# Selective-scan recurrence on one Trainium2 core: two products with B and a rounding step handed from VectorE to GpSimd, a ring of eight states written in place

## The reference, cut to what matters

```
dt  = softplus(dt_low @ dt_proj_w.T + dt_proj_b)
dA  = exp(dt[..., None] * A)
dBx = dt[..., None] * Bc[:, :, None, :] * xc[..., None]
h   = dA_t * h + dBx_t                     # for each pixel t in turn
ys  = einsum('bds,bs->bd', h, C_t)
y   = (ys + D * xc) * silu(z)
```

## Time and profile before

| | us |
|---|---|
| median of 3 runs | 5907.59 |
| lowest, highest | 5905.54, 5909.15 |
| profiled execution | 5915.02 |
| span of the profiled execution | 5913.3 |

### The profile page before, as it was taken

One profiled execution on the slowest core, in us unless ns is written; L12 is line 12 of the kernel. 1 busy time (PEld: TensorE's weight loads), 2 busy tenths in 40 slices (PEclk: granted clock), 3 DMA queues, 4 the chain that ended last, 5 costly groups with the idle time before them and its releaser, 6 DMA issues. The chain is left out here.

```text
span 5913.3 us, 100635 instructions
## 1 busy us (share of the span) xinstructions
PE 4687.3 (79%) x33816; PEld 1950.2 (33%) x33880; DVE 5095.8 (86%) x6562; ACT 3659.2 (62%) x4769; POOL 1753.6 (30%) x1306
## 2 busy tenths in 40 slices
PE   5776779998667777999866677799986667779997
PEld 2222433333322243333432224333343222433334
DVE  6799769998779977999877997799986899679998
ACT  1666458883266646888326663688922666368892
POOL 3388600000148860000014885000001488500000
PEclk9899989999889998999888999899988899989998
DMA  1000020000000002000000000200000000020000
GB/s 38 0 1 0 15 62 9 9 5 22 22 0 1 0 15 62 9 9 5 22 22 0 1 0 15 62 9 9 5 22 22 0 1 0 15 62 9 9 5 15
DMA packets 41626, 87.14 MB, mean 15 GB/s; under 512 B 11672, under 2 KB 27872, under 8 KB 38112
## 3 DMA queue, kind: packets, MB, share of 16 engines
q1 hardware_dynamic: 41184, 81.11, 5.1%
HBM read 26.55 MB, written 8.39 MB: 6 GB/s over the span
## 5 line engine op out<-in xcount | busy, mean ns | idle before, releaser
L1271 ACT ACTIVATE arena<-ps 128x1024 f32<-128x1024 f32 x2048 | 1913.2, 1027 | 266.8 <-PE ps L1236 246.4
L1286 DVE TENSOR_TENSOR arena<-arena 128x1024 f32<-128x1024 f32 x1664 | 1904.7, 1216 | 42.7 <-ACT arena L1271 40.6
L916 DVE TENSOR_TENSOR_SCAN arena<-ps,hlast,arena 128x512 f32<-128x512 f32 x1024 | 1258.4, 1264 | 5.2 <-DVE arena L898 3.2
L876 POOL TENSOR_TENSOR arena<-arena 128x1024 f32<-128x1024 f32 x512 | 1206.3, 2356 | 22.6
L1236 PE MATMUL ps<-arena 128*32 128x512 f16 x16384 | 1096.7, 384 | 118.1 <-issue 92.9
L1219 PE MATMUL ps<-arena 128*32 128x512 f32 x8192 | 1079.6, 605 | 45.9 <-DVE arena L1291 38.1
L845 ACT ACTIVATE ps<-arena,amat 128x512 f32<-128x512 f32 x1024 | 691.9, 688 | 506.9 <-DVE arena L916 506.1
L813 PE MATMUL ps<-arena,ident 128*128 128x512 f32 x2048 | 973.1, 598 | 7.7 <-POOL arena L876 7.7
L1594 POOL MEMSET arena<- 128x1024 f32 x4 | 3.8, 956 | 2688.1 <-POOLq L101 2688.1
L1236 PEld LDWEIGHTS ps<-arena 128*32 128x32 f16 x16384 | 471.4, 98 | 974.3 <-issue 696.7
L898 DVE TENSOR_TENSOR arena<-arena,ps 128x1024 f32<-128x1024 f32 x512 | 609.9, 1191 | 50.3 <-remote 32.3
(11 more groups left out here) (242 smaller groups left out, 4409.5 us busy)
## 6 DMA issues: line engine op xcount, KB each, us to landing
arena<-x SPq DMA_DIRECT2D x32, 512.0 KB, 5.5
arena<-arena SPq DMA_DIRECT2D x64, 256.0 KB, 6.0
arena<-arena SPq DMA_DIRECT2D x64, 224.0 KB, 5.8
arena<-arena SPq DMA_DIRECT2D x28, 512.0 KB, 3.4
arena<-pe SPq DMA_DIRECT2D x256, 32.0 KB, 1.8
out<-arena SPq DMA_DIRECT2D x8, 1024.0 KB, 3.9
expw<-L_ffn_expert_w SPq DMA_DIRECT2D x1, 512.0 KB
wqkv<-L_attn_W_qkv SPq DMA_DIRECT2D x1, 192.0 KB
```

The lines of the kernel that those rows point to most:

```text
L876: pool.tensor_tensor(halves(g[s % 4]), halves(hb[s % 4]), cs[s % 4].unsqueeze(1).broadcast_to([128, HD, CH]), ALU.mult).then_inc(hc_s, 1)
L916: dve.tensor_tensor_scan(halves(hb[s % 4])[:, h, :], da(s, h), halves(dbx[s % 2])[:, h, :], k.hlast[:, s, h, :], ALU.mult, ALU.add).then_i ...
L1271: act.activation(probs[p % 8], k.bank(2 * group[p], 2 * CH), ACT.Exp, scale=SCALE / SPLIT ** 2).then_inc(exp_s, 1)
L1286: dve.tensor_tensor(acc[p % 2], acc[p % 2], probs[p % 8], ALU.add).then_inc(acc_s, 1)
```

## The change

- `hb` becomes a ring of eight, and GpSimd writes h * C over the state itself; the ring `g` is gone. TensorE's `total` lags six states (`LATE`) instead of four, and C is spread and copied two states late (`CLATE`).
- States 8 and 14 (`LOANED`) get their u * B from GpSimd: TensorE spreads B into `C_BANK` at states 2 and 6, ScalarE copies it to SBUF, GpSimd multiplies at states 2 and 9 into buffers of their own. VectorE makes the other 14.
- The rounding leaves VectorE: ScalarE makes 1 - (1 + e) at state 3 and GpSimd adds e. GpSimd's softplus has four parts, at states 4, 6, 8 and 11; the logarithm is at state 6.
- ScalarE copies the last columns, two states late. `finish` is at state 4.

```
-        self.rest = self.onep[:, 0:CH]
+        self.rest = take(CH)
...
-        act.wait_ge(self.pc_s, c + 1)
         act.activation(self.onep, self.ab, ACT.Identity, bias=self.k.cols[:, C_ONE:C_ONE + 1]).then_inc(self.w_s, 1)
+    def scalar_one_minus(self, act, c, q):
+        act.wait_ge(self.w_s, c + 1)
+        act.activation(self.dt[q], self.onep, ACT.Identity, scale=-1.0, bias=self.k.cols[:, C_ONE:C_ONE + 1]).then_inc(self.m_s, 1)
...
     def scalar_log(self, act, c):
-        act.wait_ge(self.q_s, c + 1)
+        act.wait_ge(self.w_s, c + 1)
         act.activation(self.onep, self.onep, ACT.Ln).then_inc(self.ln_s, 1)
...
-    def vector_rounding(self, dve, c):
-        dve.wait_ge(self.w_s, c + 1)
-        dve.scalar_tensor_tensor(self.ab, self.onep, 1.0, self.ab, ALU.subtract, ALU.subtract).then_inc(self.q_s, 1)
...
     def pool_softplus(self, pool, c, q, part):
         if part == 0:
+            self.pool_wait(pool, self.m_s, c + 1)
+            pool.tensor_tensor(self.dt[q], self.ab, self.dt[q], ALU.add).then_inc(self.q_s, 1)
+        if part == 1:
+            self.pool_wait(pool, self.q_s, c + 1)
             self.pool_wait(pool, self.ln_s, c + 1)
-            pool.tensor_tensor(self.onep, self.onep, self.ab, ALU.subtract).then_inc(self.l1_s, 1)
-        if part == 1:
+            pool.tensor_tensor(self.dt[q], self.onep, self.dt[q], ALU.add).then_inc(self.l1_s, 1)
+        if part == 2:
             self.pool_wait(pool, self.l1_s, c + 1)
             self.pool_wait(pool, self.rx_s, c * 2 + 2)
-            pool.tensor_tensor(self.dt[q], self.onep, self.rx, ALU.add).then_inc(self.dt_s, 1)
-        if part == 2:
+            pool.tensor_tensor(self.dt[q], self.dt[q], self.rx, ALU.add).then_inc(self.dt_s, 1)
+        if part == 3:
             self.pool_wait(pool, self.dt_s, c * 2 + 1)
             pool.tensor_tensor(halves(self.u[q]), halves(self.dt[q]), self.xc[:, :, cols_of(c)], ALU.mult).then_inc(self.dt_s, 1)
...
+            steps.scalar_one_minus(act, 0, 0)
...
-            steps.vector_rounding(dve, 0)
...
-    dbx, hb, g = low[0:2], low[2:6], low[6:10]
+    dbx, hb = low[0:2], low[2:10]
+    RING, LATE, CLATE = len(hb), 6, 2
...
+    bs = [low[12][:, i * CH:(i + 1) * CH] for i in range(2)]
+    dbp = [k.at(steps.end + i * HD * CH, HD * CH) for i in range(2)]
...
+    LOANED = {8: (2, 2), 14: (6, 9)}
+    SOFTPLUS = (4, 6, 8, 11)
...
             def total(c, s):
-                pe.wait_ge(hc_s, c * DS + (s + 5))
+                pe.wait_ge(hc_s, c * DS + (s + 1))
                 if s == 0:
                     pe.wait_ge(fin_s, c + 1)
                     for h in range(HD):
...
                 for h in range(HD):
-                    last = pe.matmul(k.bank(Y_BANK + h), k.ident[:, :], halves(g[s % 4])[:, h, :], start=False, stop=s == DS - 1)
+                    last = pe.matmul(k.bank(Y_BANK + h), k.ident[:, :], halves(hb[s % RING])[:, h, :], start=False, stop=s == DS - 1)
...
+            def spread_c(c, s, q):
+                if s >= 1 or not first(c):
+                    pe.wait_ge(cs_s, c * DS + s)
+                pe.matmul(k.bank(C_BANK), k.sel[:, DS + s, :], pieces[q], start=True, stop=True).then_inc(c_mm, 1)
...
                 for s in range(DS):
                     n = c * DS + s
-                    pe.wait_ge(dbx_s, n + 1)
-                    pe.matmul(k.bank(B_BANK), k.sel[:, s, :], pieces[q], start=True, stop=True).then_inc(b_mm, 1)
-                    pe.wait_ge(cs_s, n + 1)
+                    if s not in LOANED:
+                        pe.wait_ge(dbx_s, c * OWN + (owned(s) + 1))
+                        pe.matmul(k.bank(B_BANK), k.sel[:, s, :], pieces[q], start=True, stop=True).then_inc(b_mm, 1)
+                    if s - 1 in spread_at:
+                        pe.wait_ge(lent_s, lent(c, spread_at[s - 1]) + 1)
                     if more and 1 <= s <= HD:
                         pe.wait_ge(rx_s, c * HD + (s + HD))
-                    pe.matmul(k.bank(C_BANK), k.sel[:, DS + s, :], pieces[q], start=True, stop=True).then_inc(c_mm, 1)
-                    if s >= 4:
-                        total(c, s - 4)
+                    if s >= CLATE:
+                        spread_c(c, s - CLATE, q)
                     elif not first(c):
-                        total(c - 1, s - 4 + DS)
+                        spread_c(c - 1, s - CLATE + DS, 1 - q)
+                    if s >= LATE:
+                        total(c, s - LATE)
+                    elif not first(c):
+                        total(c - 1, s - LATE + DS)
+                    if (s < HD and not first(c)) or s in spread_at:
+                        pe.wait_ge(cs_s, n + (1 - CLATE))
                     if more and s < HD:
-                        pe.wait_ge(cs_s, n + 2)
                         steps.tensor_dt(pe, c + 1, s)
+                    if s in spread_at:
+                        pe.matmul(k.bank(C_BANK), k.sel[:, spread_at[s], :], pieces[q], start=True, stop=True).then_inc(lent_mm, 1)
             chunks(body, pe)
-            for s in range(DS - 4, DS):
+            for s in range(DS - CLATE, DS):
+                spread_c(NCH - 1, s, 1)
+            for s in range(DS - LATE, DS):
                 total(NCH - 1, s)
...
+            def copy_c(c, s):
+                n = c * DS + s
+                act.wait_ge(c_mm, n + 1)
+                if s >= 4 or not first(c):
+                    act.wait_ge(hc_s, n - 3)
+                act.activation(cs[s % 4], k.bank(C_BANK), ACT.Copy).then_inc(cs_s, 1)
...
                     for h in range(HD):
                         act.wait_ge(sc_s, c * (2 * DS) + (2 * s + h + 5))
                         act.activation(da(s, h), halves(dt[q])[:, h, :], ACT.Exp, scale=k.amat[:, h, s:s + 1]).then_inc(da_s, 1)
-                    act.wait_ge(c_mm, n + 1)
-                    act.wait_ge(hc_s, n + 1)
-                    act.activation(cs[s % 4], k.bank(C_BANK), ACT.Copy).then_inc(cs_s, 1)
-                    if more and s == 0:
-                        steps.scalar_high(act, c + 1, 1 - q)
+                    act.activation(k.hlast[:, (s - 2) % DS, :, :], halves(hb[(s - 2) % RING])[:, :, CH - 1:CH], ACT.Copy).then_inc(hl_s, 1)
+                    if s >= CLATE:
+                        copy_c(c, s - CLATE)
+                    elif not first(c):
+                        copy_c(c - 1, s - CLATE + DS)
+                    if s in spread_at:
+                        p = spread_at[s]
+                        act.wait_ge(lent_mm, lent(c, p) + 1)
+                        act.wait_ge(lent_dbx, lent(c, p) + 1)
+                        act.activation(bs[loans.index(p) % 2], k.bank(C_BANK), ACT.Copy).then_inc(lent_s, 1)
                     if more and s < HD:
                         steps.scalar_abs(act, c + 1, s)
                     if more and s == 2:
+                        steps.scalar_high(act, c + 1, 1 - q)
                         steps.scalar_exp(act, c + 1)
                     if more and s == 3:
+                        steps.scalar_one_plus(act, c + 1)
+                        steps.scalar_one_minus(act, c + 1, 1 - q)
+                    if more and s == 5:
                         steps.scalar_middle(act, c + 1, 1 - q)
-                    if more and s == 7:
-                        steps.scalar_one_plus(act, c + 1)
-                    if more and s == 10:
+                    if more and s == 6:
                         steps.scalar_log(act, c + 1)
+            act.wait_ge(k.sem("h_zero"), 3)
             chunks(body, act)
+            for s in range(DS - CLATE, DS):
+                copy_c(NCH - 1, s)
...
                 for s in range(DS):
                     wait(sc_s, c * (2 * DS) + (2 * s + 2 + 8))
-                    pool.tensor_copy(k.hlast[:, s, :, :], halves(hb[s % 4])[:, :, CH - 1:CH]).then_inc(hl_s, 1)
-                    wait(cs_s, c * DS + (s + 2))
-                    wait(y_mm, c * DS + (s + 1))
-                    pool.tensor_tensor(halves(g[s % 4]), halves(hb[s % 4]), cs[s % 4].unsqueeze(1).broadcast_to([128, HD, CH]),
+                    wait(cs_s, c * DS + (s + 1))
+                    if more or s < DS - 2:
+                        wait(hl_s, c * DS + (s + 3 + DS - 2))
+                    pool.tensor_tensor(halves(hb[s % RING]), halves(hb[s % RING]), cs[s % 4].unsqueeze(1).broadcast_to([128, HD, CH]),
                                        ALU.mult).then_inc(hc_s, 1)
-                    if more and s == 0:
+                    if s in inject_at:
+                        p = inject_at[s]
+                        wait(lent_s, lent(c, p) + 1)
+                        pool.tensor_tensor(halves(dbp[loans.index(p) % 2]), halves(u[q]), bs[loans.index(p) % 2].unsqueeze(1).broadcast_to([128, HD, CH]),
...
+                    if more and s == 1:
...
-                    if more and s in (10, 11, 12):
-                        steps.pool_softplus(pool, c + 1, 1 - q, (10, 11, 12).index(s))
...
+                    if more and s in SOFTPLUS:
```

(57 more changed lines are left out.)

16 lines of the change are left out of this document (6 added, 10 removed).

## The result

The changed kernel takes 5916.2 us (median of 20 runs, 5909.6 to 5921.8), the kernel before on the same chip 5908.5 (20 runs, 5896.4 to 5911.9). The ratio is 1.0014, with a 95% interval of 1.0008 to 1.002: slower by 0.14%, where the forecast had 29 us less. The work that was to leave VectorE left, and none of it shows in the time.

What follows compares the result with a forecast made beforehand. VectorE was taken to bound the recurrence. Per batch -25.6 (work removed) + 16.2 (ScalarE wait) + 2.9 (tail) - 1.9 (start) + 1.1 (projection) = -7.3; four batches -29, from 5907.6 to 5879 us; range 5812 to 5921.

Steps and rivals of the forecast that it cites:

- Part 1: Recurrence: VectorE loses products with B and roundings, 25.6 us per batch, 102 us for four batches.
- Part 2: Recurrence: GpSimd takes the moved work, 2.29 us per large operation, 52.6 of a 54.8 us chunk, under the bound.
- Rival (b): Recurrence: GpSimd becomes the bound at the next chunk's u, slower; 5916 us at 2.43 per product, up to 6027; 13%.
- rival (a): Recurrence: the wait in ScalarE's queue does not arise; -23.5 us per batch, 5814 us; 17%.
- Part 3: ScalarE's queue: waiting for the lent matmul before the logarithm delays state 7's scan 2.35 us; 16.2 per batch with state 9's.
- Another 0.1 comes from state 9's B matmul: Full chunks: TensorE holds state 9's B matmul behind the spreading of C(6), costing VectorE 0.1 us.
- the price of chunk 0: Chunk 0: D matmuls and total take 3.5 us; state 7's scan waits 1.5; earlier B matmul waits shrink 1.9.
- Part 5: Ends, per batch: tail +2.9 us, waits for B's matmul in chunk 0 -1.9, projection +1.1.
- The tail: End of the recurrence: six totals behind the last spreading, finish 7.9 us after the last scan instead of 5.0, +2.9.
- The projection: Stage before the recurrence: one more ScalarE activation where VectorE idles for ScalarE, +1.1 us per batch.
- part 4: Recurrence: GpSimd meets the deadline for the next chunk's u by 0.2 us; wait 0, bounds 0 to 1.5.
- (c): Recurrence: break-even, half to one microsecond more wait per chunk from unseen releases, 21 us over the sum, 5900; 13%.

Runs made afterwards that it cites:

- Experiment 1: Changed kernel with the lent B matmul of state 14 and its ScalarE copy moved from state 6 to state 8, behind the logarithm: 5806.2 us, 0.983 of before.
- Experiments 1 and 2: The second is the changed kernel with ScalarE's logarithm at state 6 put ahead of its wait for the lent matmul: 5803.4 us, 0.982 of before.
- Experiment 5: Changed kernel plus fifteen unused spreading matmuls on TensorE at state 8 of chunks 1 to 7, filling its idle time: 5908.3 us, 1.0008 of before.
- experiment 7: Changed kernel with B's matmuls of states 9 and 15 issued in the turns of states 8 and 14, before the totals: 5889.2 us, 0.9971 of before.
- experiment 3: Changed kernel with nothing lent, VectorE making all 16 products with B again: 5912.6 us, 1.0006 of before.

## Why the prediction was wrong, point by point

**Part 1 held:** 24.7 us of VectorE's work less in the first recurrence for 25.6, 99 us in all four for 102.

**Part 2 and 4 held:** the products take 2.348 in place, the lent ones 2.35; u comes 1.1 before its deadline where 0.2 was forecast, since the waits leave it more time. GpSimd is busy 414.7 of 480.1 us, 86% and not the "over 90%" that was to show. Rival (b) is excluded for this kernel: no wait of VectorE in the first recurrence ends with GpSimd. That (b)'s price at 2.43, 5916, is the measured time is chance. Experiment 1, which is rival (a) made to happen, has GpSimd just at the limit, and its 5806 is near (a)'s 5814. So (a) had the right price, but its condition, that the wait does not arise, was not met.

**Part 3 held for state 7:** 2.2 us for 2.35 in the full chunks, and ScalarE's chain to it within 0.05 us at each step. That the sum of seven is right to 0.1 (15.7 for 15.6) is in part luck, since the full chunks have 0.8 less and chunk 0 has 2.47 for 1.5. Experiments 1 and 2 undo it in two ways and both give back over 100 us of the recurrence.

**What failed is part 3's "Another 0.1 comes from state 9's B matmul", and the price of chunk 0.** The first measured 1.4 in the mean of six chunks. Its cause was named rightly, TensorE holding B's matmul behind the late spreading of C(6). The size was not: all durations were taken from stretches at the full clock, a total at 1.83 and a spreading matmul at 0.38. The same edit makes TensorE idle for 3.5 us right before them, and the granted clock behind that is 0.66 in the chunk shown. Experiment 5 keeps the clock at 1.00 with matmuls in the gap, and the wait is gone; its first chunk 0 shows the same with the gap left open. What brings the clock down behind one gap and not behind another stays open.

For chunk 0 the forecast took the D matmuls and a total at 3.5 us, from the full clock. They took 5.7, at a granted clock of 0.50 in 250 to 255 us. The trace of the kernel before had the rows for it: it too is at 0.50 in 232 to 251 us, its D matmuls take 3.62 there (246.69) and the total 2.30 (250.11), and state 5's product waits 1.07 behind them. Part 5 took that wait for one of the dt matmuls', whose two are 0.92 and 1.54. So the waits in chunk 0 did not shrink by 1.9: those two went, the third has its like in the 1.40 before state 7's product, and 1.99 came. No run isolates the 1.40. The last chunk, set at 0, has one of 1.3, behind D matmuls of 2.80 and a total of 2.77.

**The sum of the first batch** comes out so, from the first product to the last finish: 472.3 us before (232.28 to 704.59), 475.3 after (232.91 to 708.22), +3.0. Forecast for the recurrence: -25.6 + 16.2 + 2.9 - 1.9 = -8.4. VectorE's work is -24.7 and not -25.6, +0.9. The waits for B's matmul go from 3.5 to 13.2, +9.7, where the sum had 0.6 - 1.9 = -1.3, so +11.0. State 7's are 15.7 for 15.6, +0.1. The tail is +2.5 (7.4 for 4.9) and not +2.9, -0.4; smaller waits are 0.2 less. Together -8.4 + 11.4 = +3.0. All four, by stage: 1913.6 to 1919.0.

In the 1913.6 the second batch has 481.4 where the others have 477.4. There the clock falls in the kernel before as well: at 1952.76 us, behind an idle time of 1.90, to 0.66 for 5 us, and the next product with B waits 1.31. Such waits make 7.3 us in that recurrence and 3.5 in the first, from which all rows of the prediction came.

**The projection:** its stage is 281.1 for 283.4, so -0.6 a batch and not +1.1. The activation came; its cost is hidden. The two medians are 7.7 us apart; in the one profile of each the recurrence has 5.4 more. The rest is smaller than attention's own spread.

The range reaches to 5921 and so takes in 5916, but by luck: its upper end is 1.5 more a chunk, the bound of part 4 for GpSimd, which did not occur. What was wrong is the likeliest value, by 37 us, and the chances with it: waits that had not been seen, (c), had 13% and a price of 0.75 a chunk, half of what state 9 alone cost.

## What to carry to other kernels

A wait that an edit puts into an in-order queue costs what stands behind it; look there first for the slow thing, here a table load, a logarithm and a table load, and let that go before the wait. When an edit makes TensorE idle for some microseconds, do not price the matmuls behind it from rows at the full clock alone; look in all batches of the trace for rows that follow such idle times, count how often the clock fell, and give the case in which it falls a price. The same holds for a stretch that starts at half the clock, as chunk 0 does. Filling the gap removed the wait here, and yet the device time did not clearly fall. And once VectorE has been relieved, ask which engine is next: here GpSimd was within one instruction a chunk of the bound.

## What the runs showed of the hardware

A short idle time of TensorE can cost again behind itself. In the changed kernel each of the 28 idle times of about 3.5 us was followed by 5 us at a granted clock of 0.50 to 0.71, in a stretch that from chunk 1 on is otherwise mostly at 1.00. Matmuls there took 0.63 for 0.38, and four of a total 2.69 (3.62 in chunk 0) for 1.88. With fifteen matmuls of no use in the gap, the windows stayed at 1.00 and the four took 1.88.

The length of the gap alone does not decide it. Behind idle times of 3.27 us in experiment 7 the clock stayed at 1.00 in 12 of 28 cases and fell to between 0.50 and 0.73 in the others. Behind 1.6 to 2.0 us, met at the full clock, it fell in 24 of 28 cases in experiment 3 and in 3 of 28 in the kernel before. What else decides it was not found.

A stage that no edit touched, attention, differed by up to 40 us between the profiled executions of these kernels.
